# GpSimd waits for the landing of a chunk's gathers before it starts the next chunk's: four gather loops and a scatter loop on one core

## The reference

```
x = layernorm(x + L0(x))   # h = x @ W; agg[dst] += h[src] * deg_out[src]**-0.5 * deg_in[dst]**-0.5; + b
x = layernorm(x + L1(x))   # twice: msg = x[src] @ Wm + edge_attr @ We; agg = segment_max(msg, dst);
                           #        leaky_relu(agg + x @ Wr + b)
x = layernorm(x + L2(x))   # m = relu(x[src]) + eps; softmax of m over the edges of a node, per feature;
                           #        (x + sum(a * m)) @ W + b
x = layernorm(x + L3(x))   # h = x @ W; e = leaky_relu(h[src].att_src + h[dst].att_dst), self loops added;
                           #        softmax over the edges of a node; tanh(sum(alpha * h[src]) + bias)
```

## Time and profile before

| | |
|---|---|
| median of 3 runs | 5194.56 us |
| the profiled execution's own time | 5199.31 us |
| its span (first to last instruction) | 5197.6 us |
| busy: POOL / DVE / PE / ACT | 52% / 52% / 41% / 40% of the span |
| granted PE clock, mean | 0.596 of full speed |
| DMA moved | 524.77 MB, mean 101 GB/s |

### The profile page before, as it was taken

The page is one execution under the profiler, slowest core; times in us unless marked ns, Lnnn a source line. Parts: engine busy times, 40 slices in busy tenths (PEclk is TensorE's granted clock), DMA queues, the critical chain, the costliest instruction groups (busy, mean ns, idle before and its releaser), DMA issues. The chain is left out here.

```text
span 5197.6 us, 42938 instructions
## 1 busy us (share of the span) xinstructions
PE 2116.6 (41%) x9550; PEld 1627.5 (31%) x9550; DVE 2726.6 (52%) x10673; ACT 2077.1 (40%) x4598; POOL 2688.3 (52%) x2760
## 2 busy tenths in 40 slices
PE   5111584544555557766455452667862000000000
PEld 2000241144445546665333331556761000000000
DVE  8300695655555545555467665667763343434344
ACT  9100691044444411111233333455654444534444
POOL 6677004144445355554455554455644656566564
PEclk9555895567767666566555555566555555555555
DMA  1111004833333445544345554344432222222221
GB/s 54 44 40 35 5 1 120 223 89 100 106 102 100 109 133 156 158 154 152 115 150 160 154 154 128 116 135 151 158 119 67 66 61 64 64 60 68 56 70 41
DMA packets 361451, 524.77 MB, mean 101 GB/s; under 512 B 221626, under 2 KB 230607, under 8 KB 360938
## 3 DMA queue, kind: packets, MB, share of 16 engines
q1 hardware_dynamic: 267050, 366.82, 21.3%
q0 software_dynamic: 94144, 155.21, 13.0%
HBM read 230.29 MB, written 291.54 MB: 100 GB/s over the span
## 5 line engine op out<-in xcount | busy, mean ns | idle before, releaser
L1938 POOL DMA_INDIRECT out<-O,nidx x392 | 385.1, 983 | 375.9 <-ACT O L207 257.1
L1623 POOL DMA_INDIRECT l_G<-t,src x391 | 382.2, 978 | 318.3 <-issue 287.6
L1303 POOL DMA_INDIRECT l1a_G<-t,src x391 | 376.7, 963 | 308.5 <-issue 274.9
L1303 POOL DMA_INDIRECT l1b_G<-t,src x391 | 381.6, 976 | 295.0 <-issue 271.8
L642 POOL DMA_INDIRECT O<-x_pad,nidx x344 | 338.5, 984 | 373.1 <-PE en_psB L841 263.9
L2163 PE MATMUL l_psR<-l_diag,l_ones 128*128 128x128 f32 x2 | 0.8, 502 | 1241.8 <-DVE l_diag L2016 1241.8
L973 POOL DMA_INDIRECT l_G<-xs,src x327 | 313.2, 958 | 363.4 <-DVE l_G L1004 248.5
L1923 POOL DMA_INDIRECT l_G<-t,src x391 | 375.2, 960 | 169.2 <-issue 118.9
L2163 PEld LDWEIGHTS l_psR<-l_diag,l_ones 128*128 128x128 f32 x2 | 0.5, 313 | 1241.8 <-DVE l_diag L2016 1241.8
L1501 PE MATMUL l1a_psP<-l1a_w,l1a_xT 97*128 97x192 f32 x784 | 250.6, 507 | 216.8 <-ACT l1a_xT L1418 157.3
L1480 PE MATMUL l1b_psE<-l1b_we,l1b_edge 32*128 32x96 f32 x782 | 197.6, 430 | 304.1 <-DMA l1b_edge<-edge_k 260.4
(11 more groups left out here) (347 smaller groups left out, 6752.3 us busy)
## 6 DMA issues: line engine op xcount, KB each, us to landing
h<-l_G SPq DMA_DIRECT2D x96, 392.0 KB, 2.4
t<-l1b_t_out SPq DMA_DIRECT2D x48, 768.0 KB
h<-l_G SPq DMA_DIRECT2D x48, 768.0 KB
xs<-en_y SPq DMA_DIRECT2D x48, 392.0 KB
t<-l_t_out SPq DMA_DIRECT2D x48, 392.0 KB
l_H<-t SPq DMA_DIRECT2D x48, 392.0 KB
en_y<-x_pad SPq DMA_DIRECT2D x48, 384.0 KB
t<-l_tr_out SPq DMA_DIRECT2D x48, 384.0 KB
```

Of the source, the lines that this page charges most:

```text
L1303: pool.indirect_dma_start(tile(c)[:, q, :], None, table, bass.IndirectOffsetOnAxis(k.src[:, at:at + 1], 0))\
L1623: pool.indirect_dma_start(tile(c)[:, q, :], None, table, bass.IndirectOffsetOnAxis(k.src[:, at:at + 1], 0))\
L1938: pool.indirect_dma_start(out, bass.IndirectOffsetOnAxis(k.nidx[:, at:at + 1], 0), k.O[:, at, :], None, bounds_check=NP - 1, oob_is_err=Fa ...
```

## The change

In each of the four gather programs POOL waits, ahead of a chunk's 8 gathers, for the landing of the chunk ahead of it. In layer 3 the wait stands in `scatter` instead: ahead of the scatter of chunk c, POOL waits for the landing of the gathers of chunk c+2, which it has just issued. The parts after the last full chunks (c of 49 and 50; in `scatter` c + 2 of 49 and more) and layer 0's first gathered chunk have no such wait. No instruction is removed and no DMA changed.

```diff
@@ layer 0
             for c in range(RAW, NL):
                 s = c % SLOTS
+                if RAW < c < NCH:
+                    pool.wait_ge(gathered.of(c - 1), gathered.by(c - 1))
                 if SLOTS <= c < NCH:
                     pool.wait_ge(turned_s, fours(c - SLOTS + 1))
@@ layer 1 (both) and layer 2, the same text in each
             for c in range(NL):
                 s = c % SLOTS
+                if 1 <= c < NCH:
+                    pool.wait_ge(gathered.of(c - 1), gathered.by(c - 1))
                 if SLOTS <= c < NCH:
                     pool.wait_ge(joined, c - SLOTS + 1)
@@ layer 3
             def scatter(c):
                 u = c % 2
+                if c + 2 < NCH:
+                    pool.wait_ge(gathered.of(c + 2), gathered.by(c + 2))
                 pool.wait_ge(normed, c + 1)
                 for q in range(width(c)):
```

## The result

The changed kernel takes **4806.43 us** (median of 4 runs, 4790.8 to 4853.64) where the kernel before takes 5187.45 (4 runs beside it, 5177.83 to 5202.66): ratio **0.928 [0.921, 0.935]**. The forecast was 4790 (4670 to 5080), with 0.87 for faster. Within a session the runs of one kernel lie within 2% of each other, but for three slow ones in the sessions of the second kind (4285 us for the kernel before, 4402 and 3894 for two of the variants), from which nothing is read.

What follows compares the result with a forecast made beforehand. Bound: engines standing still during POOL's long DMA runs, not throughput or buffers. Loop gains of 139, 5, 51, 67 and 114 us (376) plus 30 for ends make 406 off 5199.31: 4793, stated as 4790, range 4670 to 5080.

Steps and rivals of the forecast that it cites:

- The standstill: All loops: other engines stop late in POOL's long DMA runs; a pause of some 2 us after 8 DMAs avoids it.
- The rival by which DRAINs last by the operation ahead of them: Layer 3: DVE's pauses are its own, so POOL's waits change nothing; within 25 us of 5195, no-effect chance 0.05.
- The price of one wait: Each chunk's wait on POOL: 2.1 us added, low bound 1.4, high bound 3.6.
- the slower rival: All loops: landing 4.05 us after the last gather, so each wait adds 4.6 us; 156 us slower, 5350; chance 0.08.
- Layer 0 was mis-sized: Layer 0: tick from 15.6 to 12.2 us, gaining 139 us, or 149 with its share of the ends.
- the half relief of the rival: All loops: runs of 8 already suffer at their end, each wait adds 3.6 us; 80 us gained, 5115; chance 0.13.
- 1a was mis-sized: Loop 1a: tick from 13.3 to 13.2 us, since its gap on POOL hides the wait; 5 us gained.
- the something faster: Loop 1a: relieved as well, tick 12.3 for 13.2 us, 45 us more gained; the rest of the chances.
- The ends: Ends of layers 0, 1b and 2: others one chunk behind POOL instead of three; 30 us gained in all.
- 1b and layer 2: Ticks from 13.3 and 13.7 to 12.3 us, gaining 51 and 67; 61 and 77 with shares of the ends.
- Layer 3: Layer 3: tick 22.5 us with runs of 16 DMAs, 1080 us for 1194, gaining 114.
- the late `normed`: Layer 3: if it ticks at 24 us because `normed` comes late, DVE and ACT set its tick and the forecast is wrong.

Runs made afterwards that it cites:

- h1: The changed kernel with each wait for the chunk two ahead, so POOL hardly pauses: 5148.99 us, ratio 0.999 to the kernel before (5147.96).
- e3_lag2: The changed kernel with each wait for the chunk two ahead, run where the kernel before takes 3809.88 us: 3810.16 us, ratio 1.000.
- e1_gather_only: The changed kernel without layer 3's scatter wait, run where the kernel before takes 3809.88 us: 4130.35 us, ratio 1.083.
- g2_contig: The changed kernel with layer 0's two outputs in contiguous halves, run where the kernel before takes 3804.14 us: 4216.04 us, ratio 1.109.
- i1_contig_again: The changed kernel with layer 0's two outputs in contiguous halves, run again where the kernel before takes 3815.7 us: 4221.91 us, ratio 1.107.
- the second pair of traces: The changed kernel and the kernel before, both unmodified, run and profiled again: 4762.18 us against 5172.29, ratio 0.921.

## Why the prediction was right, point by point

**The standstill.** Right for the condition in which the kernel before had been profiled: in the loops it comes and goes with POOL's unbroken runs. Pauses end it in three loops and shorten it in two; the same waits without pauses (h1) do nothing. DVE's idle time behind layer 0's run of DMAs fell from 12.56 to 4.26 us. The rival by which DRAINs last by the operation ahead of them falls too: layer 3 got shorter with every instruction of DVE's unchanged (10673 of them, 2726.6 us of busy time before and 2724.0 after). One DRAIN of layer 3, behind the same operation of 0.17 us, by min/median/max in ns, in the held trace before and in e3_lag2's free one:

```profile
L1979 DVEq DRAIN  x51: 171/1954/8760, 3945.5 to 5162.2; - x51
```

```profile
L1987 DVEq DRAIN  x51: 156/173/1912, 2786.6 to 3764.3; - x51
```

What inside the chip holds the engines, and that it is completions that don't arrive, is my reading of such rows and not shown. One more difference goes with the condition: the held traces have 22,374 to 27,510 updates of semaphores on record, the free ones some 67,000. Whether the lost records and the standstill have one cause stays open too.

**The price of one wait.** 2.1 us added, forecast; in 1a 2.35 us of waiting at each, the 0.30 of the usual gap in it, so 2.05 added; 2.0 in 1b. In layer 2 it was less, 93.7 / 48 = 1.95 and so 1.65 added, but there each gather took 1.05 us instead of 0.98, and the tick came out at 12.4 for 12.3. That was the sum's most sensitive term and outside layer 0 it held, but only by the 1.65 us of one landing, not by the 5.0 of the earlier trace rows, from which the slower rival came. The trace after has 4.6 for its one printed landing, and e3_lag2's trace, where most completions are recorded, has medians of 2.2 to 2.6 us from issue for every POOL line of the loops but layer 1's gathers (4.4), so some 1.6 us behind the end of the DMA's own 0.95; for layer 0's gathers its line reads

```profile
DMA to landing us min/median/max: 2.5/2.6/2.6
```

A line with a single event is no typical one. The Trainium skill ("DMA: Bandwidth & Descriptors", Anatomy of one DMA) gives about 2.0 us of fixed cost for GpSimd's DMAs; that is 0.2 to 0.6 us less than those medians.

**Layer 0 was mis-sized**: 81 gained for 149. The step that failed is "A run of 8 ends 10 us after its start, before the stretch in which layer 0 stands still". Engines stop there for the last 2.4 us of the run (DVE from 1449.61 on) and the landing comes after 3.75 us, so the tick is about 13.7 ((1665.9 - 1105.6) / 40.9) and not 12.2. That is the half relief of the rival, in this one loop, though not by its reason. The landing is late because the gathers' own data are late. In the stretches of 3 us the DMA engines are full just when POOL has stopped (share 1.01), while in the free session (e1_gather_only, second fence) such a burst falls into the middle of a run:

```profile
1449.00:1452.00 3.00, 0.50 (x5) 0.25 (x3) 0.53 (x3) 0.57 (x1) 2.39 (x3) 1.00 0.59 138
1452.00:1455.00 3.00, 0.34 (x2) 0.36 (x3) 1.13 (x5) 1.07 (x2) 0.03 (x1) 0.51 1.01 322
```

```profile
900.00:903.00 3.00, 3.00 (x14) 2.47 (x13) 2.76 (x13) 1.86 (x4) 2.13 (x3) 0.50 1.05 292
```

```profile
908.02 0.94 POOL L975 DMA_INDIRECT l_G<-xs,src  x1 [1.82 <-DMA l_G<-xs,src]
```

The burst is SP's stores of layer 0, issued from 1449.60 us on. By the DMA packets of the same trace no packet of a gather starts from 1451 to 1453 us, and those of the two last gathers follow until about 1455. (In the free session none starts from 900 to 902 us either, but there the run goes on behind it.) Over the 40 waits of this loop the last packet of a chunk ends 2.9 us (median) after POOL's last DMA, and POOL goes on 0.8 us after that packet; in e1_gather_only it is 1.2 and 0.6 us. The trace has 41 gaps between chunks here. In 27 of them the last packet ends more than 1.6 us after POOL's last DMA, and each of these has 437 or more store packets in it, most some 1900; the 14 others have 136 at the most, most of them none. In e1_gather_only 3 of 41 are late, and these too have stores in them. So small packets alone don't make the landing late, and a withheld completion doesn't either; the burst does, where it meets the end of a run. Why it meets it so often in a held session, and whether larger packets would cure it, stays open: g2_contig and i1_contig_again, made for that, met free sessions.

**1a was mis-sized the other way**: 76 gained for 5. I took the 13.25 us of the earlier trace rows, with POOL waiting 3.4 us per chunk, for the loop's undisturbed pace, set by others than POOL. But those rows are from a stretch of a few chunks. Over most of 1a, in the same trace, chunks take some 10.4 and 17.3 us in turn, as in 1b, and only their mean is near 13.3:

```profile
2085.76 0.94 POOL L1303 DMA_INDIRECT l1a_G<-t,src  x1 [0.61 <-issue]
...
2102.99 0.95 POOL L1303 DMA_INDIRECT l1a_G<-t,src  x1 [7.36 <-issue]
...
2113.48 0.95 POOL L1303 DMA_INDIRECT l1a_G<-t,src  x1 [0.62 <-issue]
```

So the standstill was there to be cut as well: 1a ticks at (2309.8 - 1715.4) / 48.9 = 12.2 after, the something faster that I gave the rest of the chances, and at 10.1 in e3_lag2, where PE does the same work. A tick read from one stretch has to be held against the whole loop's starts, and not only against its mean.

**The ends** were too small a term. From the last gather of a loop to the next loop's first (the last: to the end of the span) 3.6 us were gained in layer 0, 19.9 in 1a, 10.1 in 1b, 20.0 in layer 2 and 0.3 in layer 3: 53.9 where I had 30. From first to last gather the gains are 77.7, 56.5, 61.2, 61.0 and 82.9: 339.3 where I had 376.

**1b and layer 2**: 71 and 81 for 61 and 77. Ticks 12.1 and 12.4 for 12.3, right; the rest is in the ends. For layer 2 the second pair of traces gives only 50.5, because the kernel before was faster there.

**Layer 3**: 83 for 114. Reckoned as in the sum, with the scatters that the first two chunks don't have, the tick is (4734.5 - 3623.2 + 20.6) / 48.9 = 23.1 against 22.5. With the same waits it is (4166.0 - 3094.2 + 20.6) / 48.9 = 22.3 in i1_contig_again's free session, so the price was right and the 31 us are standstill that was left: the step that failed is "the stretch from 20 us on, where DVE does a quarter of its work, is cut off". It is left in runs of 16 that still have a stretch at their end where DVE does less (10.6, 8.8 and 6.7 us in 20, by stretch, where e3_lag2 has 9.9 in each), and in chunks where `normed` comes late: 84.5 us in 12 waits of POOL on ACT. DVE's pauses are fewer and not gone: between the loop's first and last gather 85 of its DRAINs last over 2.5 us before, 22 after, none in e3_lag2. I had named the late `normed` as what would make me wrong, and the gap of over 3.5 us and the standstill inside runs of 8 as well; the last two came true in layer 0.

So 4790 for 4806 is luck in part: it rests on two errors of some 70 us that cancel (68 too much in layer 0, 71 too little in 1a), while 31 too much in layer 3 is half made up in 1b and layer 2. And the step that no row of one condition could have shown: that a wait's gain depends on a standstill that isn't always there. In a free session my forecast's sign would have been wrong: the whole change never met one as it stands, but its gathers' waits did (1.083 and 1.085), and so did all its waits together with the other layout of the stores (1.109 and 1.107). The rival's mechanism for slower, a wait dearer than what it cuts, is what happens there, though not by its reason: the wait isn't dearer (1.74 us); there is no standstill to cut.

## What to carry to other kernels

Where several engines fall idle together and come back together just after a long run of GpSimd's DMAs, the engines' work isn't the bound; a wait of some 2 us for the landing after every 8 of them was worth 7 to 8% here. It helped only where GpSimd really paused at it: the same waits for the chunk two ahead gained nothing. Whether it is the idle time or the empty queue that helps is not shown. Where the standstill is absent the wait costs its length at each place: so look first at a stretch that no change touches (here the 710 or 430 us of the setup's gathers) to see in which condition a run was, and measure in both before keeping such a change.

## What the runs showed of the hardware

- One program, two times: 5148 to 5187 us or 3804 to 3816, by session; the DMAs' own durations on POOL are the same in both (median 944 to 949 ns, and 1007 and 1009 for layer 2's gathers in the kernels with the waits) and the granted clock is about 0.60 or 0.64 of full speed. Both were met under one chip number, eleven minutes apart. What switches it stays open.
- In a held session 64 gathers in a row (5 to 104 us) leave the others at work (DVE 42.7 of the first 50 us, 42.3 in a free one). In the next run, of 344, the others stop some 20 DMAs in (DVE 2.7 us of 50, against 44.7), and it takes 710 us (157 to 867) against 430.
- In the two places shown the others came through 1.8 us after the end of a run of 8 DMAs and 3.1 us after one of 16. With 8 in a row DVE still stood idle for 4.3 us at the end of a run in layer 0, while 1a, 1b and layer 2 took no longer than in a free session.
- A DRAIN behind an operation of 0.17 us lasted up to 8.8 us in the held trace before, and up to 1.9 us in a free one.
- A burst of SP's stores (DMA share 1.01, 322 GB/s over 3 us) that met the end of a run of gathers let their last packet end 2.9 us after the last issue, instead of 1.2.
- In layer 0 of a free session POOL went on 1.8 us after the end of a run's last DMA, landing and restart included. A wait for the landing costs 1.74 us net in the mean of the gather loops and 2.1 in the scatters.
